# Layernorm, token-shift feed-forward and retention for 4096 tokens on one core: keys and values from one product, the token shift scaled by ScalarE

## The chip, the core and the metric

The kernel runs on one core of a Trainium2 chip. The metric is device time in microseconds, the median of the runs. A core has five engines that run their own instruction streams and wait for one another by semaphores: TensorE (PE in the profile; its weight loads are PEld), VectorE (DVE), ScalarE (ACT), GpSimd (POOL) and SyncE (SP), which starts the transfers.

## What is computed

x has 4096 tokens of 256 channels, in fp32. Three layers follow one another, each on the layernorm of its input (no gain, no bias) and added to it:

```python
x = x + 0.5 * ffn(layernorm(x))      # W_r, W_k, W_v, mu_r, mu_k
x = x + retention(layernorm(x))      # Wq, Wk, Wv, Wo, 8 heads of 32
x = x + 0.5 * ffn(layernorm(x))      # the same weights again

def ffn(x):                          # x_prev: the token before, zeros first
    xr = mu_r * x + (1.0 - mu_r) * x_prev
    xk = mu_k * x + (1.0 - mu_k) * x_prev
    r = sigmoid(xr @ W_r.T)
    return r * (square(relu(xk @ W_k.T)) @ W_v.T)
```

Retention is linear attention with a decay per head: within a chunk, scores q k^T are masked to the past and decayed and multiplied by v; a state of 32x32 per head carries the earlier chunks; the result goes through Wo.

## The kernel before

**Blocks and layers.** Tokens go in 16 blocks of 256 (TILES = 2 tiles of 128). Each block n passes the layers FFN1, RET and FFN2, which are staggered: in the steady loop (i from 6 to 15) TensorE works on FFN1 of one block, RET of a block two or three earlier and FFN2 of one earlier still. Chunks of the retention are 128 tokens, two per block (c = 0, 1).

**One layer's way.** VectorE takes the statistics (layer_stats), GpSimd the inverse deviation (inverse_std), ScalarE normalizes (normalize, L295), TensorE transposes (transpose_T, L890) so that channels lie on partitions, and ScalarE copies the result out of PSUM (evacuate_T, L302, with the last token of the block before as a halo, L305). For the token shift VectorE forms the difference of neighbouring tokens (difference, L536) and from it xk and xr (mix_k L545, mix_r L552: difference times mu plus the earlier token).

**Products in three passes.** Each fp32 operand is split in a high part in the reduced format fp32r and a low part with the rest (xk_high on ScalarE, xk_low on VectorE, xr_low on GpSimd L213, and so on), and a product is high x high + low x high + high x low. A half of a product is six matmuls with 256 columns, which half_T (L893) and half_rows (L901) issue: hidden, gate, ffn_out, query, key, value and retention_out each have two halves per block.

**Retention.** query and key come out with channels on partitions; VectorE scales the queries (decayed_query), ScalarE copies the keys to kT (evacuate_key). key_rows transposes kT back to rows, which VectorE scales to krow (decayed_key). value gives rows, which ScalarE copies to vrow (evacuate_value). scores (L976), each four row groups of 32 at once, are multiplied by a decay table (mask_scores, L607), intra (L1003) multiplies them by vrow, inter (L990) the queries by the state, outer (L1013) krow by vrow for the new state. Then o_high, o_low, retention_out, add_retention.

**Order.** Every engine's program is written out by hand as a list of such steps, with a start, the steady loop and an end; engines run their lists strictly in order. All eight PSUM banks are shared by several steps (B_T, B_HID and so on), and a step waits where its bank is still to be read. Loads of x, weights and tables are issued by SyncE at the start, stores as results come.

## Time and profile before

| | |
|---|---|
| median of 3 runs | 350.52 us (349.65 to 351.63) |
| the profiled execution | 349.89 us |
| its span, first to last instruction | 347.7 us |
| busy: PE, DVE, ACT, POOL | 325.6, 302.5, 211.5, 162.3 us |
| mean granted clock of TensorE | 0.990 |

Busy is the time in which at least one instruction of the engine ran. A matmul's record reaches beyond the start of the next one, since matmuls are pipelined; the rate is read from starts, not from the duration. An activation's or vector operation's record, too, can overlap the next one's start.

### The profile page before, as it was taken

What the parts mean: (1) busy time and instruction counts of PE and PEld (TensorE: products, weight loads), DVE (VectorE), ACT (ScalarE), POOL (GpSimd) and SP (SyncE); (2) the same over time, 40 slices, a digit from 0 to 9 for tenths busy, and PEclk for the clock granted to TensorE, in tenths of its full rate; (3) what the DMA queues carried; (4) which work ended last, traced back from release to release, by engine and by line L of the source; (5) the groups of instructions that cost most, each with busy time, mean ns of one, the idle gap of its engine ahead of it and who ended that gap; (6) DMA issues with size and microseconds to landing.
All of it is one profiled execution on the core that took longest, in us unless ns stands there. A gap on an engine that the chain in (4) does not pass through costs nothing.

```text
span 347.7 us, 10332 instructions
## 1 busy us (share of the span) xinstructions
PE 325.6 (94%) x3858; PEld 313.3 (90%) x3858; DVE 302.5 (87%) x695; ACT 211.5 (61%) x418; POOL 162.3 (47%) x271
## 2 busy tenths in 40 slices
PE   1969999899999999999999999999999999999774
PEld 1859999899999999999999999999999999999674
DVE  3898997999899998989899898989999897898744
ACT  3675557567667657657657757657756656545342
POOL 4384463435627281744727282653736181414130
PEclk9999999999999999999999999999999999999969
DMA  7601000000102020200202020100000000000001
GB/s 251 228 30 31 5 32 2 31 4 17 46 3 62 2 62 2 65 0 4 60 3 62 2 61 3 41 23 32 3 7 27 2 32 2 33 2 32 33 0 60
DMA packets 11664, 12.15 MB, mean 35 GB/s; under 512 B 992, under 2 KB 11232, under 8 KB 11616
## 3 DMA queue, kind: packets, MB, share of 16 engines
q1 hardware_dynamic: 11328, 11.44, 10.6%
q8 instruction: 31, 0.51, 0.6%
q14 instruction: 17, 0.14, 0.1%
q10 hardware_dynamic: 288, 0.07, 0.1%
HBM read 7.31 MB, written 4.19 MB: 33 GB/s over the span
## 4 chain that ended last, share of the span: by engine, by line
PE 85%; issue 6%; DVE 4%; POOL 2%; ACT 1%; DMA 1%; POOLq 0%; DVEq 0%; ACTq 0%
PE bank L906 36%; PE bank L898 24%; PE bank L890 6%; PE bank L976 5%; PE bank L990 5%; PE bank L1003 4%; PE bank L966 2%; PE bank L1013 2%; PE bank L1027 1%; DMA x<-in_x 1%; DVE stats L525 1%; POOL xr_lo L213 1%; POOL rstd L206 1%; DVE xk_lo L557 1%; DVE xrT L552 0%
## 5 line engine op out<-in xcount | busy, mean ns | idle before, releaser
L213 POOL TENSOR_TENSOR xr_lo<-xrT,xr_hi 128x512 fp32r<-128x512 f32 x32 | 54.3, 1697 | 95.4 <-ACT xr_hi L315 94.2
L295 ACT ACTIVATE xn<-x,shift,rstd 128x256 f32<-128x256 f32 x96 | 52.2, 593 | 12.4 <-POOL shift L209 12.4
L222 POOL TENSOR_TENSOR state_bd<-state,mask 128x256 f32<-128x256 f32 x32 | 28.6, 893 | 45.9 <-DVE state L621 43.9
L890 PE MATMUL bank<-ident,xn 128*128 128x128 f32 x192 | 30.5, 283 | 12.6 <-ACT xn L295 12.6
L607 DVE TENSOR_TENSOR attn<-bank,decay 128x512 f32<-128x512 f32 x64 | 40.5, 678 | 1.0 <-PE bank L976 0.4
L906 PE MATMUL bank<-w_hi,xr_hi 128*128 128x256 f32 x128 | 39.4, 308 | 0.4 <-POOL xr_lo L213 0.4
L525 DVE BATCH_NORM_STATS2 stats<-x 128x6 f32<-128x256 f32 x96 | 35.7, 414 | 4.6 <-DMA x<-in_x 4.4
L898 PE MATMUL bank<-xk_hi,w_hi 128*128 128x256 f32 x128 | 38.2, 299 | 0.9 <-DVE xk_lo L557 0.9
L906 PE MATMUL bank<-w_hi,ka_hi 128*128 128x256 f32 x128 | 36.8, 288 | 2.1 <-DVE ka_lo L563 2.1
L202 POOL TENSOR_TENSOR var_eps<-moments,eps 128x2 f32<-128x2 f32 x48 | 20.7, 431 | 38.3 <-DVE moments L529 38.1
L898 PE MATMUL bank<-xa_hi,w_hi 128*128 128x256 f32 x128 | 36.8, 287 | 0.0
L906 PE MATMUL bank<-w_lo,xr_hi 128*128 128x256 f32 x128 | 36.3, 284 | 0.0
L906 PE MATMUL bank<-w_hi,xr_lo 128*128 128x256 f32 x128 | 36.3, 284 | 0.0
L906 PE MATMUL bank<-w_lo,ka_hi 128*128 128x256 f32 x128 | 36.0, 281 | 0.0
L906 PE MATMUL bank<-w_hi,ka_lo 128*128 128x256 f32 x128 | 36.0, 281 | 0.0
L898 PE MATMUL bank<-xk_hi,w_lo 128*128 128x256 f32 x128 | 35.7, 279 | 0.0
L898 PE MATMUL bank<-xa_lo,w_hi 128*128 128x256 f32 x128 | 35.6, 278 | 0.0
L898 PE MATMUL bank<-xa_hi,w_lo 128*128 128x256 f32 x128 | 35.6, 278 | 0.0
L898 PE MATMUL bank<-xk_lo,w_hi 128*128 128x256 f32 x128 | 35.6, 278 | 0.0
L890 PEld LDWEIGHTS bank<-ident,xn 128*128 128x128 f32 x192 | 22.7, 145 | 13.7 <-issue 12.1
L206 POOL TENSOR_TENSOR rstd<-var_eps,exponent 128x2 f32<-128x2 f32 x48 | 33.6, 700 | 0.0
L570 DVE SCALAR_TENSOR_TENSOR gatedx<-bank,rgate 128x512 f32<-128x512 f32 x32 | 22.0, 687 | 12.6 <-PE bank L906 12.5
(80 smaller groups left out, 1068.4 us busy)
## 6 DMA issues: line engine op xcount, KB each, us to landing
x<-in_x SPq DMA_DIRECT2D x16, 256.0 KB, 3.0
x_out<-y SPq DMA_DIRECT2D x16, 256.0 KB, 2.6
w_f<-in_w SPq DMA_DIRECT2D x7, 256.0 KB, 5.2
decay<-in_decay SPq DMA_DIRECT2D x1, 512.0 KB, 6.3
decq<-in_decq SPq DMA_DIRECT2D x1, 256.0 KB, 5.8
deck<-in_deck SPq DMA_DIRECT2D x1, 256.0 KB, 6.0
mask<-in_mask SPq DMA_DIRECT2D x1, 128.0 KB, 5.5
ident<-in_ident ACTq DMA_DIRECT2D x1, 64.0 KB, 2.6
```

The costliest lines, as they stand in the source:

```text
L202: pool.tensor_tensor(var_eps[s][n % 2][:], m[:, :, 1], eps[:], ALU.add).then_inc(var_ready[s], 1)
L206: pool.tensor_tensor(rstd[s][n % 2][:], var_eps[s][n % 2][:], exponent[:], ALU.pow).then_inc(rstd_ready[s], 1)
L213: pool.tensor_tensor(xr_lo[f][n % 2][:], xrT[f][n % 2][:], xr_hi[f][n % 2][:].bitcast(F32), ALU.subtract).then_inc(xr_lo_ready[f], 1)
L222: pool.tensor_tensor(state_bd[1 - c][:], state[c][:].unsqueeze(2).broadcast_to([P, G, HG, HD]), mask[:], ALU.mult).then_inc(state_bd_ready ...
L295: act.activation(xn[s][n % 2][:, t, :], x[n % len(x)][:, t, :], ACT.Identity, bias=shift[s][n % 2][:, t:t + 1], scale=rstd[s][n % 2][:, t: ...
L525: dve.bn_stats(stats[s][n % 2][:, t, :], x[n % len(x)][:, t, :]).then_inc(stats_ready[s], 1)
L570: dve.scalar_tensor_tensor(out=gatedx[f][0][:], in0=halves(B_OUT[f]), scalar=0.5, in1=rgate[f][0][:], op0=ALU.mult, op1=ALU.mult).then_inc ...
L607: dve.tensor_tensor(attn[r][:], bank[B_SCORES[r]][:].rearrange("p (g c i) -> p g c i", g=G, c=TILES), decay[:, r, :, :].unsqueeze(2).broad ...
L890: mm = pe.transpose(halves(B_T[s])[:, g, t * P:(t + 1) * P], xn[s][n % 2][:, t, g * P:(g + 1) * P], ident[:])
L898: mm = pe.matmul(halves(b)[:, m, :], wt[:, g, cols], xt[:, g, :], start=(j == 0), stop=(j == 5))
L906: mm = pe.matmul(halves(b)[:, t, :], xt[:, g, cols], wt[:, g, :], start=(j == 0), stop=(j == 5))
L976: mm = pe.matmul(bank[B_SCORES[r]][:, group * P:(group + 1) * P], kT[rows, g, c * P:(c + 1) * P], qT[rows, g, c * P:(c + 1) * P], start=Tr ...
```

## The change

Keys and values are computed by one product: their weights lie side by side (wkv_hi, wkv_lo, 512 columns), and key_value streams 512 columns in each of 2 x 6 matmuls per block, into two adjacent banks, one per tile. Keys now come out as rows. VectorE scales them to krow first (decayed_key), ScalarE then copies the values (evacuate_value waits for krow_ready), and key_T transposes krow to kT, so that the scores already hold the decay of the keys; mask_scores multiplies by a causal table of zeros and ones [128, 128] instead of a decay table per head.

For the token shift ScalarE forms mu * x for both mixes out of PSUM (scale_k, scale_r: two activations of 128x256 each), beside the plain copy; VectorE's difference is gone, and mix_k and mix_r are (1 - mu) times the earlier token plus that product. mu_rest = 1 - mu is computed once on GpSimd.

PSUM banks are assigned anew, and all four engines' orders are new. Which engine splits which weight at the start has changed too. relu also waits for ka_hi_ready of the block before. At the start ScalarE's list begins split_high_act(W_K), normalize(FFN1, 0), evacuate_T, scale_k, scale_r (all FFN1, 0), normalize(FFN1, 1); TensorE's is hidden(0) both halves, gate(0, 0), hidden(1, 0), gate(0, 1), ffn_out(0). At the end the copy of xnT of block 15 is followed by scale_k and scale_r. The new steady loops of GpSimd, ScalarE, VectorE and TensorE (in this order, each under its own `for i in range(6, 16)`) are shown below, the last three without the lines that they replace.

```diff
-        w_hi = [sb(f"w_hi_{w}", [G, D], F32R) for w in range(7)]
-        w_lo = [sb(f"w_lo_{w}", [G, D], F32R) for w in range(7)]
+        w_hi = [None if w in (W_KEY, W_VAL) else sb(f"w_hi_{w}", [G, D], F32R)[:] for w in range(7)]
+        w_lo = [None if w in (W_KEY, W_VAL) else sb(f"w_lo_{w}", [G, D], F32R)[:] for w in range(7)]
+        wkv_hi, wkv_lo = sb("wkv_hi", [G, 2 * D], F32R), sb("wkv_lo", [G, 2 * D], F32R)
+        for side, w in enumerate((W_KEY, W_VAL)):
+            w_hi[w] = wkv_hi[:, :, side * D:(side + 1) * D]
+            w_lo[w] = wkv_lo[:, :, side * D:(side + 1) * D]
...
-        B_T = {FFN1: 4, RET: 1, FFN2: 5}
-        B_HID, B_GATE, B_OUT = {FFN1: 0, FFN2: 4}, {FFN1: 2, FFN2: 2}, {FFN1: 6, FFN2: 7}
-        B_Q, B_KEY, B_VAL, B_KROW = 7, 5, 3, 5
-        B_SCORES = (4, 7, 6, 1)
-        B_OT, B_U, B_Y = 5, (3, 0), 3
+        B_T = {FFN1: 7, RET: 4, FFN2: 6}
+        B_HID, B_GATE, B_OUT = {FFN1: 2, FFN2: 3}, {FFN1: 1, FFN2: 0}, {FFN1: 5, FFN2: 2}
+        B_Q, B_KV, B_KEYT = 1, 6, 7
+        B_SCORES = (4, 3, 7, 5)
+        B_OT, B_U, B_Y = 0, (1, 5), 0
...
+        def keys_values(which):
+
+            return psum[:, B_KV:B_KV + TILES, :].rearrange("p t (k c) -> p t k c", k=2)[:, :, which, :]
+
...
             for i in range(6, 16):
                 inverse_std(FFN1, i)
-                spread_state(0, i - 4)
+                spread_state(1, i - 4)
                 xr_low(FFN2, i - 5)
+                xr_low(FFN1, i - 1)
                 inverse_std(FFN2, i - 4)
-                xr_low(FFN1, i - 1)
                 inverse_std(RET, i - 2)
-                spread_state(1, i - 4)
+                spread_state(0, i - 3)
...
+            def scale_k(f, n):
+                if n == 0:
+                    act.wait_ge(mu_loaded, 16)
+                act.wait_ge(xnT_psum[f], n + 1)
+                act.wait_ge(xk_ready[f], max(2 * (n - 1), 0))
+                for g in range(G):
+                    act.activation(akT[f][n % 2][:, g, :], halves(B_T[f])[:, g, :], ACT.Copy, scale=mu[:, 1, g:g + 1]).then_inc(ak_ready[f], 1)
+
+            def scale_r(f, n):
+                if n == 0:
+                    act.wait_ge(mu_loaded, 16)
+                act.wait_ge(xnT_psum[f], n + 1)
+                act.wait_ge(xr_ready[f], max(2 * (n - 1), 0))
+                for g in range(G):
+                    act.activation(arT[f][n % 2][:, g, :], halves(B_T[f])[:, g, :], ACT.Copy, scale=mu[:, 0, g:g + 1]).then_inc(ar_ready[f], 1)
+
...
             def xa_high(n):
                 act.wait_ge(xnT_psum[RET], n + 1)
-                act.wait_ge(val_psum, n)
+                act.wait_ge(q_psum, n)
                 act.activation(xa_hi[:], halves(B_T[RET]), ACT.Copy).then_inc(xa_hi_ready, 1)
 
             def evacuate_key(n):
-                act.wait_ge(key_psum, n + 1)
+                act.wait_ge(keyT_psum, n + 1)
                 act.wait_ge(scores_psum, HG * n)
-                act.activation(kT[:], halves(B_KEY), ACT.Copy).then_inc(key_ready, 1)
+                act.activation(kT[:], halves(B_KEYT), ACT.Copy).then_inc(key_ready, 1)
 
             def evacuate_value(n):
-                act.wait_ge(val_psum, n + 1)
+                act.wait_ge(krow_ready, n + 1)
                 act.wait_ge(u_psum[1], n)
                 act.wait_ge(intra_done, n)
-                act.activation(vrow[:], halves(B_VAL), ACT.Copy).then_inc(val_ready, 1)
+                act.activation(vrow[:], keys_values(1), ACT.Copy).then_inc(val_ready, 1)
...
             for i in range(6, 16):
+                evacuate_value(i - 4)
+                relu(FFN2, i - 6)
+                square(FFN2, i - 6)
+                square_high(FFN2, i - 6)
+                evacuate_key(i - 4)
+                relu(FFN1, i - 2)
+                normalize(FFN2, i - 5, x2)
+                square(FFN1, i - 2)
+                sigmoid(FFN2, i - 6)
+                square_high(FFN1, i - 2)
+                evacuate_T(FFN2, i - 5)
+                scale_k(FFN2, i - 5)
+                normalize(RET, i - 3, x1)
+                xk_high(FFN2, i - 5)
+                o_high(i - 4)
+                scale_k(FFN1, i - 1)
+                xa_high(i - 3)
+                scale_r(FFN2, i - 5)
+                evacuate_T(FFN1, i - 1)
+                scale_r(FFN1, i - 1)
+                xr_high(FFN2, i - 5)
+                sigmoid(FFN1, i - 2)
+                xk_high(FFN1, i - 1)
                 normalize(FFN1, i, x0)
                 xr_high(FFN1, i - 1)
...
             def mix_k(f, n):
+                dve.wait_ge(ak_ready[f], 2 * n + 2)
                 dve.wait_ge(xnT_ready[f], n + 1)
                 dve.wait_ge(halo_ready[f], n)
                 dve.wait_ge(xk_lo_ready[f], max(n - 1, 0))
                 for g in range(G):
-                    dve.scalar_tensor_tensor(out=xkT[f][n % 2][:, g, :], in0=dT[f][n % 2][:, g, :], scalar=mu[:, 1, g:g + 1],
-                                             in1=xnT[f][n % 2][:, g, 0:BT], op0=ALU.mult, op1=ALU.add).then_inc(xk_ready[f], 1)
+                    dve.scalar_tensor_tensor(out=xkT[f][n % 2][:, g, :], in0=xnT[f][n % 2][:, g, 0:BT], scalar=mu_rest[:, 1, g:g + 1],
+                                             in1=akT[f][n % 2][:, g, :], op0=ALU.mult, op1=ALU.add).then_inc(xk_ready[f], 1)
 
             def mix_r(f, n):
-                dve.wait_ge(d_ready[f], n + 1)
+                if n == 0:
+                    dve.wait_ge(halo_zeroed, 2)
+                    dve.wait_ge(mu_rest_set, 1)
+                dve.wait_ge(ar_ready[f], 2 * n + 2)
+                dve.wait_ge(xnT_ready[f], n + 1)
+                dve.wait_ge(halo_ready[f], n)
                 dve.wait_ge(xr_lo_ready[f], max(n - 1, 0))
                 for g in range(G):
-                    dve.scalar_tensor_tensor(out=xrT[f][n % 2][:, g, :], in0=dT[f][n % 2][:, g, :], scalar=mu[:, 0, g:g + 1],
-                                             in1=xnT[f][n % 2][:, g, 0:BT], op0=ALU.mult, op1=ALU.add).then_inc(xr_ready[f], 1)
+                    dve.scalar_tensor_tensor(out=xrT[f][n % 2][:, g, :], in0=xnT[f][n % 2][:, g, 0:BT], scalar=mu_rest[:, 0, g:g + 1],
+                                             in1=arT[f][n % 2][:, g, :], op0=ALU.mult, op1=ALU.add).then_inc(xr_ready[f], 1)
 
 ...
             def decayed_key(n):
                 if n == 0:
                     dve.wait_ge(deck_loaded, 16)
-                dve.wait_ge(krow_psum, n + 1)
-                dve.wait_ge(u_psum[0], n)
+                dve.wait_ge(kv_psum, TILES * n + TILES)
                 dve.wait_ge(u_psum[1], n)
-                dve.tensor_tensor(krow[:], halves(B_KROW), deck[:], ALU.mult).then_inc(krow_ready, 1)
+                dve.tensor_tensor(krow[:], keys_values(0), deck[:], ALU.mult).then_inc(krow_ready, 1)
 
             def mask_scores(r, n):
                 if n == 0:
-                    dve.wait_ge(decay_loaded, 16)
+                    dve.wait_ge(causal_loaded, 16)
                 dve.wait_ge(scores_psum, HG * n + r + 1)
                 dve.wait_ge(intra_done, n)
-                dve.tensor_tensor(attn[r][:], bank[B_SCORES[r]][:].rearrange("p (g c i) -> p g c i", g=G, c=TILES),
-                                  decay[:, r, :, :].unsqueeze(2).broadcast_to([P, G, TILES, P]), ALU.mult).then_inc(attn_ready[r], 1)
+                dve.tensor_tensor(attn[r][:], bank[B_SCORES[r]].rearrange("p (k i) -> p k i", i=P),
+                                  causal[:].unsqueeze(1).broadcast_to([P, G * TILES, P]), ALU.mult).then_inc(attn_ready[r], 1)
...
+            for i in range(6, 16):
                 add_retention(i - 5)
                 scale_state(0, i - 4)
+                xk_low(FFN1, i - 2)
+                decayed_key(i - 4)
                 layer_stats(FFN2, i - 5, x2)
                 add_ffn1(i - 3)
                 decayed_query(i - 4)
                 layer_stats(RET, i - 3, x1)
                 square_low(FFN2, i - 6)
+                mask_scores(2, i - 4)
+                update_state(0, i - 4)
+                mask_scores(0, i - 4)
+                mask_scores(1, i - 4)
+                mask_scores(3, i - 4)
                 layer_stats(FFN1, i, x0)
                 mix_k(FFN2, i - 5)
+                scale_state(1, i - 4)
+                gate(FFN2, i - 6)
+                update_state(1, i - 4)
+                square_low(FFN1, i - 2)
+                xk_low(FFN2, i - 5)
+                o_low(i - 4)
+                xa_low(i - 3)
+                mix_r(FFN2, i - 5)
+                mix_k(FFN1, i - 1)
+                mix_r(FFN1, i - 1)
+                add_ffn2(i - 6)
+                gate(FFN1, i - 2)
...
+            def key_value(n, t):
+
+                if n == 0:
+                    weight_split(n, W_KEY)
+                    weight_split(n, W_VAL)
+                pe.wait_ge(xa_lo_ready, n + 1)
+                cols = slice(t * P, (t + 1) * P)
+                passes = [(xa_hi, wkv_hi), (xa_hi, wkv_lo), (xa_lo, wkv_hi)]
+                for j, (g, (xt, wt)) in enumerate([(g, p) for g in range(G) for p in passes]):
+                    mm = pe.matmul(bank[B_KV + t], xt[:, g, cols], wt[:, g, :], start=(j == 0), stop=(j == 5))
+                mm.then_inc(kv_psum, 1)
+
+            def key_T(n):
+                pe.wait_ge(krow_ready, n + 1)
+                for g in range(G):
+                    for c in range(TILES):
+                        mm = pe.transpose(halves(B_KEYT)[:, g, c * P:(c + 1) * P], krow[:, c, g * P:(g + 1) * P], ident[:])
+                mm.then_inc(keyT_psum, 1)
...
             for i in range(6, 16):
                 pe.wait_ge(gated[FFN2], i - 5)
+                hidden(FFN1, i - 1, 0)
+                pe.wait_ge(krow_ready, i - 2)
+                pe.wait_ge(val_ready, i - 2)
+                key_T(i - 3)
+                query(i - 3, 1)
+                pe.wait_ge(xout_ready[RET], i - 3)
+                gate(FFN2, i - 5, 0)
+                hidden(FFN1, i - 1, 1)
+                pe.wait_ge(xa_lo_ready, i - 2)
                 pe.wait_ge(relu_ready[FFN2], i - 4)
+                pe.wait_ge(key_ready, i - 2)
+                pe.wait_ge(gated[FFN1], i - 1)
+                scores(i - 3, 1, first=True)
+                scores(i - 3, 3)
+                scores(i - 3, 2)
+                scores(i - 3, 0, last=True)
+                pe.wait_ge(q_ready, i - 2)
+                outer(0, i - 3)
+                gate(FFN2, i - 5, 1)
+                pe.wait_ge(krow_ready, i - 2)
+                pe.wait_ge(val_ready, i - 2)
+                transpose_T(FFN2, i - 4)
+                pe.wait_ge(attn_ready[2], i - 2)
                 transpose_T(FFN1, i)
+                pe.wait_ge(relu_ready[FFN1], i)
+                ffn_out(FFN2, i - 5, 0)
                 pe.wait_ge(gate_ready[FFN2], i - 4)
+                inter(0, i - 3)
+                pe.wait_ge(state_ready[0], i - 2)
                 gate(FFN1, i - 1, 0)
+                ffn_out(FFN2, i - 5, 1)
+                intra(i - 3)
+                pe.wait_ge(attn_ready[3], i - 2)
+                outer(1, i - 3)
+                inter(1, i - 3)
+                gate(FFN1, i - 1, 1)
+                pe.wait_ge(attn_ready[0], i - 2)
+                transpose_T(RET, i - 2)
+                pe.wait_ge(state_ready[1], i - 2)
+                ffn_out(FFN1, i - 1, 0)
                 pe.wait_ge(attn_ready[1], i - 2)
+                hidden(FFN2, i - 4, 0)
+                pe.wait_ge(o_lo_ready, i - 2)
+                retention_out(i - 3, 0)
+                ffn_out(FFN1, i - 1, 1)
+                pe.wait_ge(ak_ready[FFN2], 2 * (i - 3))
+                pe.wait_ge(ar_ready[FFN2], 2 * (i - 3))
                 pe.wait_ge(xnT_ready[FFN2], i - 3)
+                key_value(i - 2, 0)
+                retention_out(i - 3, 1)
+                pe.wait_ge(ar_ready[FFN1], 2 * (i + 1))
+                key_value(i - 2, 1)
+                hidden(FFN2, i - 4, 1)
+                pe.wait_ge(gate_ready[FFN1], i)
+                query(i - 2, 0)
             pe.wait_ge(gated[FFN2], 11)
```

## Rows read from the trace of the kernel before

**Rows 1.** The page's busy times and its slices of the span, TensorE's row (tenths busy in each of 40).
```profile
PE 325.6 (94%) x3858; PEld 313.3 (90%) x3858; DVE 302.5 (87%) x695; ACT 211.5 (61%) x418; POOL 162.3 (47%) x271
PE   1969999899999999999999999999999999999774
```

**Rows 2.** The page's chain of work that ended last, shares by engine.
```profile
PE 85%; issue 6%; DVE 4%; POOL 2%; ACT 1%; DMA 1%; POOLq 0%; DVEq 0%; ACTq 0%
```

**Rows 3.** Stretches: us, busy us and instructions of each engine, PE clock, DMA share, GB/s.
```profile
0.00:20.00 20.00, 10.47 (x62) 9.84 (x62) 13.19 (x29) 10.69 (x20) 9.59 (x26) 1.00 0.61 208
20.00:40.00 20.00, 17.80 (x218) 16.56 (x219) 17.48 (x42) 12.44 (x25) 11.91 (x17) 1.00 0.10 29
...
80.00:99.74 19.74, 19.74 (x242) 19.16 (x242) 18.36 (x44) 12.93 (x26) 10.23 (x16) 1.00 0.10 29
...
317.00:333.00 16.00, 11.46 (x150) 10.35 (x149) 10.96 (x23) 7.34 (x14) 4.35 (x9) 0.94 0.06 19
333.00:347.70 14.70, 10.12 (x79) 9.34 (x77) 7.05 (x14) 4.90 (x9) 2.01 (x2) 0.83 0.10 36
```

**Rows 4.** The timeline of TensorE from 182 to 202 us (start, duration).
```profile
182.01 0.60 PE L890 MATMUL bank<-ident,xn 128*128 128x128 f32 x4
...
195.01 0.60 PE L890 MATMUL bank<-ident,xn 128*128 128x128 f32 x4
195.37 0.36 PE L898 MATMUL bank<-xk_hi,w_hi 128*128 128x256 f32 x1
195.57 0.28 PE L898 MATMUL bank<-xk_hi,w_lo 128*128 128x256 f32 x1
...
200.33 0.28 PE L898 MATMUL bank<-xa_hi,w_hi 128*128 128x256 f32 x1
...
201.63 0.28 PE L898 MATMUL bank<-xa_lo,w_hi 128*128 128x256 f32 x1
201.75 0.60 PE L890 MATMUL bank<-ident,xn 128*128 128x128 f32 x4
```

**Rows 5.** The timeline of TensorE in the last block, at the lower clock.
```profile
335.01 0.41 PE L906 MATMUL bank<-w_hi,xr_hi 128*128 128x256 f32 x1
...
337.36 0.41 PE L906 MATMUL bank<-w_hi,xr_lo 128*128 128x256 f32 x1
```

**Rows 6.** Groups by line: shapes, count, busy us, mean ns, idle time before.
```profile
L295 ACT ACTIVATE xn<-x,shift,rstd 128x256 f32<-128x256 f32 x96 | 52.2, 593 | 12.4 <-POOL shift L209 12.4
...
L563 DVE TENSOR_TENSOR ka_lo<-sqT,ka_hi 128x512 fp32r<-128x512 f32 x32 | 26.0, 813 | 3.8 <-ACT sqT L324 3.3 <-ACT ka_hi L329 0.5
...
L536 DVE TENSOR_TENSOR dT<-xnT 128x512 f32<-128x512 f32 x32 | 22.0, 687 | 1.7 <-ACT xnT L305 1.0 <-ACT xnT L302 0.7
...
L302 ACT ACTIVATE xnT<-bank 128x512 f32<-128x512 f32 x32 | 19.1, 596 | 22.4 <-PE bank L890 22.3
...
L615 DVE TENSOR_TENSOR state_dec<-state,gstate 128x64 f32<-128x64 f32 x32 | 6.9, 217 | 0.1
...
L305 ACT ACTIVATE xnT<-xnT 128x2 f32<-128x2 f32 x30 | 6.1, 202 | 0.0
```

**Rows 7.** The timelines of ScalarE and VectorE in the steady loop.
```profile
196.18 1.09 ACT L295 ACTIVATE xn<-x,shift,rstd 128x256 f32<-128x256 f32 x2
197.17 0.62 ACT L310 ACTIVATE xk_hi<-xkT 128x512 fp32r<-128x512 f32 x1
...
197.08 0.68 DVE L585 TENSOR_TENSOR xa_lo<-bank,xa_hi 128x512 fp32r<-128x512 f32 x1
197.68 1.66 DVE L552 SCALAR_TENSOR_TENSOR xrT<-dT,mu,xnT 128x256 f32<-128x256 f32 x4
199.26 0.68 DVE L557 TENSOR_TENSOR xk_lo<-xkT,xk_hi 128x512 fp32r<-128x512 f32 x1
```

**Rows 8.** The timelines of ScalarE and TensorE in the last block.
```profile
331.11 1.09 ACT L295 ACTIVATE xn<-x,shift,rstd 128x256 f32<-128x256 f32 x2 [0.92 <-POOL shift L209]
...
332.34 1.09 PE L890 MATMUL bank<-ident,xn 128*128 128x128 f32 x4 [3.45 <-ACT xn L295]
```

955 lines of the change are left out of this document (420 added, 535 removed).

## The prediction

> **What bounds the kernel now.** I read the page's totals first [rows 1]: TensorE is busy for 94% of the span, VectorE for 87%, ScalarE for 61%, and TensorE's slices are full from the ninth to the 37th of 40. The chain that ended last says the same by another way: 85% of it is TensorE [rows 2]. The table of stretches then shows where that holds [rows 3]. Between 80 and 99.74 us TensorE is busy for all 19.74 us. Idle time lies at the start (9.5 us of the first 20), in the ramp (2.2 us of the next 20) and at the end (4.5 us before 333 us, 4.6 us after it). The first transposes of block 6 and those of block 7 start 19.74 us apart (182.01 and 201.75 us) [rows 4], so that one block of 256 tokens costs one period of 19.74 us, and nothing but TensorE's own stream sets it. Sixteen blocks of this are 316 of the 347.7 us. What shortens that stream is therefore worth its full size in every block, as long as no loop through the other engines becomes longer than the new period.
>
> The profiled execution took 349.89 us, 2.2 us more than its span. The sum below is made against it; the median of the runs shown, 350.52 us, lies 0.6 us above it, and I move the result by as much. I count a difference under 0.5% (1.75 us) as no change, since the three runs before already differ by 2 us.
>
> **Keys and values in one product.** Before, key and value are four halves of six matmuls with 256 columns each, 24 per block. After, key_value is twice six matmuls with 512 columns. As many columns are streamed; 12 weight loads and 12 starts fall away. In a run of twelve, the 256-column matmuls start 0.118 us apart ((201.63 - 200.33) / 11) [rows 4], where 256 columns at 2.4 GHz are 0.107 us. So 0.011 us of each is not streaming. Is it a fixed part that a matmul twice as wide pays once, not at all, or does it grow with the columns? The tail answers half of it: at a lower granted clock (0.83 in the mean of that stretch [rows 3]) eleven starts take 2.35 us, 0.2136 us each [rows 5], which is 256 columns at 1.2 GHz (0.2133) with nothing left over. The extra time vanishes when streaming lasts 0.213 us; it looks like a floor on the interval between two matmuls, not like a surcharge. 512 columns at 2.4 GHz last 0.213 us as well, so I take 0.215 us. The bounds are 0.213 us (streaming alone) and 0.236 us (all of it grows with the columns). Saved per block: 24 x 0.118 - 12 x 0.215 = 0.25 us, between 0 and 0.28; over 16 blocks 4.0 us, between 0 and 4.4.
>
> The Trainium skill (TensorE: Matmul & The Clock Gate, section "Wait — 56ns, not 53.3ns?") gives a start-to-start time of N / 2.4 GHz plus about 2.5 ns. That speaks against this change: two 256-column matmuls would take 218 ns and one of 512 columns 216 ns, a gain of 0.03 us per block and 0.5 us in all instead of 4.0. The trace does not bear it out at 256 columns (118 ns, not 109) [rows 4]; for 512 columns it agrees with what I take.
>
> **The new order on TensorE.** A group of transposes takes 0.36 us, and the first matmul after it takes 0.20 us to the next instead of 0.118 (195.01, 195.37, 195.57) [rows 4]: leaving the fp32 operations costs 0.08 us. In the new steady loop transpose_T(FFN2) and transpose_T(FFN1) stand side by side, and outer(0) behind scores; inter(0) stands alone. Counted group by group one exit less remains, some 0.1 us a block (0 to 0.15), 1 us in all. key_T replaces key_rows: four transposes for four. The new period of TensorE is 19.74 - 0.25 - 0.1 = 19.39 us.
>
> **ScalarE.** scale_k and scale_r add eight activations of 128x256 out of PSUM per block. The trace has none of the form. A copy of 128x512 out of PSUM takes 0.596 us and one of two columns 0.202, so 0.77 ns a column, and 256 columns without operands come to 0.40 us; normalize, with a scale and a bias per partition, takes 0.593 [rows 6], so each operand costs about 0.1. One operand: 0.50 us, and since two normalizations occupy the engine for 0.99 us though each lasts 0.593 [rows 7], 0.1 overlaps: 0.40 us each. Bounds: 0.30 (the operand free) and 0.50 (as normalize). That is 3.2 us more on 12.93 us of ScalarE in a period [rows 3], 16.1 of 19.39: 83%, hidden behind TensorE by load.
>
> **VectorE.** difference goes: two of 0.69 us a block [rows 6], 0.60 in a packed queue [rows 7]. mix_k and mix_r keep their form. mask_scores reads one causal table instead of a decay table per head, in the same shape; I cost it and decayed_key, which now reads two banks, at nothing, as they keep 512 elements. VectorE falls from 18.36 to 17.2 us a period, 88%; GpSimd stays where it is. These 1.2 us are worth nothing by themselves: VectorE was not the bound. The decay table, 512 KB among the first loads, shrinks to 64 KB; nothing waited on it.
>
> **The loop that could replace TensorE.** Values are now evacuated only after krow is ready, and key_T waits for both, with hidden(FFN1, 0) alone between the last query half and it. I followed the loop once round. TensorE from key_T to the end of inter(1) holds seven halves (six matmuls each) and all fp32 groups but transpose_T(RET). A half is 6 x 0.118 = 0.71 us; of the period before, 20 halves are 14.18 us, which leaves 5.56 for the fp32 groups, of which 0.44 is the group left out and 0.1 falls away: 4.96 + 5.02 = 9.98 us. Then release 0.28 (the transposes' 0.60 lasts 0.24 beyond the next start [rows 4]), o_high 0.50 (0.596 less the overlap of 0.1), scale_k(FFN1) 0.80, xa_high 0.50, scale_r(FFN2) 0.90 with its end: 3.0 us. VectorE is then packed: three mixes at 0.79 (four instructions take 1.58 [rows 7]), add_ffn2, gate and add_retention at 0.60, scale_state 0.13 (0.217 long [rows 6]), xk_low 0.60, decayed_key 0.68: 5.6 us. evacuate_value 0.60 and two handoffs, 0.14 of them from ScalarE to TensorE (332.20 to 332.34) [rows 8]: 0.8 us. Together 19.3 to 19.4 us, against 19.39 of TensorE; I take 19.3. It fits, with hardly 0.1 us to spare. The queues around it fit too: evacuate_key follows 0.8 us ahead of scores, ka_lo and xk_lo of both layers some 0.8 us ahead of their products.
>
> **Start and end.** At the start ScalarE has four more activations before normalize(1) (1.6 us), so the second transposes come 1.5 us later; but hidden(1) moves ahead of ffn_out(0), whose wait for ka_lo stood there, and counted step by step scores(0) come as early as before, within half a microsecond. I cost start and ramp at +0.5 us (-1 to +2): each early block has a longer ScalarE path and little other work to hide it. In the last block the copy of xnT is followed by scale_k (0.9) where difference (0.7) was: equal within 0.2. The wait before the last transposes (3.45 us [rows 8]) starts earlier, because o_high and o_low of block 15 no longer queue behind xk_high, the sigmoid and more; I take -0.5 us (-1.5 to +1).
>
> **Sum.** -4.0 (wide product) - 1.0 (exits) + 0.5 (ramp) - 0.5 (end) = -5.0 us: span 342.7, profiled execution 344.9, median **345.5 us**.
>
> **Rivals.** (a) The value loop sets the period and eats the gain. If a scale costs 0.50 us like a normalization, four of them lie in the loop: 19.3 + 0.4 = 19.7 us, as before. Some 12.5 periods gain 0.5 us in all, the ramp about 1: 349. For it: 0.1 us of slack. Against: the sum has one operand less than normalize. 12%.
> (b) Slower: GpSimd and VectorE disturb each other in that loop. square_low, an operation of the shape of xk_low, takes 0.81 us in the mean for 0.68 undisturbed [rows 6, 7]. xr_low of both layers now runs just while the packed VectorE part does. If three of its operations are stretched by 0.3 us, the period is 20.2 us: 0.46 x 12.5 - 1.2 = +4.5 us, 355. It decides from 0.7 us of stretch on; below 0.44 it costs only gain. 10%.
> (c) A 512-column matmul takes 0.236 us: only exits are won, 349.5. Rows 5 speak against it. 5%.
> (d) Ramp and end lose 3 to 4 us by the longer ScalarE path, for instance because TensorE waits in blocks 1 to 3: 349. 5%.
> (e) The floor between two matmuls is all that counts and a wide one takes hardly more than 0.118 us: TensorE's period would be 19.39 - 12 x 0.097 = 18.2, the value loop would hold at 19.3, and 16 x 0.44 = 7 us would go: 343.5. At the low clock a column never took less than one clock [rows 5]. 2%. The Trainium skill (same page, section "Back-to-back issue gap") states this 131 ns for 512 columns as a sustained rate; no run here shows it.
>
> **Numbers.** The forecast holds 66% and reaches from 342.5 (0.28 and 0.15 a block are 6.9 us, and 1 of the good bounds at start and end) to 348.5. To leave out 2 in 10 at most, the range goes to 350: it takes in (a), (c) and (d). Faster by over 0.5% is the forecast and (e), 68%; within it (a), (c) and (d), 22%; slower (b), 10%.
>
> **What would show it.** Matmuls of 512 columns start 0.215 us apart; periods of 19.4 us wholly filled; ScalarE near 83% and VectorE at 88% in them; scale instructions of 0.50 us; no wait of TensorE for vrow or krow at key_T. Wrong would be: a wait at key_T in every period, for ScalarE's evacuation of the values; a pitch of 0.236; or more idle time of TensorE than 22 us.

## The result: slower, by 3.6%

| | before | after |
|---|---|---|
| median | 351.07 us (349.65 to 352.94, 4 runs) | **362.60 us** (361.35 to 364.68, 4 runs) |
| ratio | | 1.0355, interval 1.0306 to 1.0404 |
| span of the profiled execution | 347.7 us | 360.7 us |
| time of the first scores of blocks 0, 2, 3, 12 | 33.99, 67.33, 87.08, 264.74 | 37.68, 71.60, 92.18, 277.63 |
| period from block 3 to 12 | 19.74 us | 20.58 us (one of 20.81) |

The ratio and its interval are those on record for these runs; the two medians alone give 1.033, which lies in the same interval. Three runs with a granted clock of 0.56 to 0.66 are left out of all times and ratios below: one of pool_apart (536.36 us), one of start_order (464.82 us) and one of the kernel before beside it (534.43 us).

The forecast was 345.5 us, range 342.5 to 350. The time lies outside it, on the side of rival (b), which had 10%.

The last two lines say where the 13.0 us of span come from: the first scores begin 3.7 us late, the ramp to block 3 adds 1.4, nine steady periods add 7.8, and from the scores of block 12 on less than 0.1 is added. So there are two losses, one ahead of block 3 and one in every period.

### The profile after

The page's busy times and TensorE's slices, to be read beside [rows 1]:

```profile
PE 332.8 (92%) x3666; PEld 309.3 (86%) x3666; DVE 303.5 (84%) x664; ACT 257.3 (71%) x546; POOL 150.0 (42%) x271
PE   1879999999999999999999999999999999999764
PEclk9998999999999999999999999999999999999988
```

In tenths the slices look as full as before; a loss of 2% in each can't be seen in them. The page's chain of work that ended last shows it at once, 60% TensorE where it was 85% [rows 2]:

```profile
PE 60%; DVE 15%; issue 13%; ACT 9%; DMA 1%; POOL 1%; DVEq 0%; ACTq 0%
```

Stretches, columns as in [rows 3]; the third is one period:

```profile
0.00:20.00 20.00, 10.60 (x56) 10.06 (x56) 10.31 (x25) 11.36 (x23) 8.99 (x26) 1.00 0.57 185
20.00:40.00 20.00, 17.33 (x149) 15.50 (x149) 15.92 (x39) 15.00 (x31) 11.01 (x20) 0.91 0.09 29
...
80.00:100.58 20.58, 20.16 (x231) 18.80 (x229) 18.91 (x42) 15.73 (x35) 9.31 (x17) 1.00 0.08 27
...
333.00:360.70 27.70, 17.23 (x164) 15.96 (x162) 14.80 (x30) 13.47 (x28) 5.89 (x8) 0.90 0.09 30
```

TensorE has 0.42 us without any instruction in the period, besides gaps hidden in the overlap of records. VectorE is busy for 18.91 us though the change took 1.2 us of work from it: it should be 17.2. The 0.91 in the second line is TensorE at 1.2 GHz from 27.6 to 31.0 us, behind a wait of 1.93 us for ka_lo that ended at 26.95.

Groups by line, columns as in [rows 6]:

```profile
L223 POOL TENSOR_TENSOR xr_lo<-xrT,xr_hi 128x512 fp32r<-128x512 f32 x32 | 42.7, 1334 | 76.2 <-ACT xr_hi L342 76.2
L608 DVE SCALAR_TENSOR_TENSOR xrT<-xnT,mu_rest,arT 128x256 f32<-128x256 f32 x64 | 40.5, 674 | 0.1
L596 DVE SCALAR_TENSOR_TENSOR xkT<-xnT,mu_rest,akT 128x256 f32<-128x256 f32 x64 | 29.2, 497 | 6.1 <-ACT akT L324 3.8 <-ACT xnT L316 2.1 <-issue 0.2
L332 ACT ACTIVATE arT<-psum,mu 128x256 f32<-128x256 f32 x64 | 27.7, 503 | 0.0
L324 ACT ACTIVATE akT<-psum,mu 128x256 f32<-128x256 f32 x64 | 26.8, 476 | 1.1 <-PE psum L902 1.1
L378 ACT ACTIVATE vrow<-psum 128x512 f32<-128x512 f32 x16 | 9.6, 598 | 42.3 <-DVE krow L655 42.3
```

The reader is to see two lines of equal form, xrT and xkT, with 674 and 497 ns: something stretches the one and not the other. ScalarE's scales last 0.48 to 0.50 us. Its wait for krow ahead of vrow is 2.6 us in each of 16 blocks; with the loop repaired (pool_apart and three_together, below) 1.4 to 1.5 us of it are left, so the late part of it is 1.2 us. VectorE's timeline where that happens, one period of 20.58:

```profile
184.68 0.88 DVE L608 SCALAR_TENSOR_TENSOR xrT<-xnT,mu_rest,arT 128x256 f32<-128x256 f32 x2
185.79 0.88 DVE L596 SCALAR_TENSOR_TENSOR xkT<-xnT,mu_rest,akT 128x256 f32<-128x256 f32 x2 [0.23 <-issue]
186.59 1.96 DVE L608 SCALAR_TENSOR_TENSOR xrT<-xnT,mu_rest,arT 128x256 f32<-128x256 f32 x2
...
190.27 0.39 DVE L670 TENSOR_TENSOR state_dec<-state,gstate 128x64 f32<-128x64 f32 x1
190.58 0.68 DVE L613 TENSOR_TENSOR xk_lo<-xkT,xk_hi 128x512 fp32r<-128x512 f32 x1
191.19 0.68 DVE L655 TENSOR_TENSOR krow<-psum,deck 128x512 f32<-128x512 f32 x1
```

and GpSimd's in the same stretch:

```profile
186.56 1.31 POOL L223 TENSOR_TENSOR xr_lo<-xrT,xr_hi 128x512 fp32r<-128x512 f32 x1 [3.61 <-ACT xr_hi L342]
189.28 1.29 POOL L223 TENSOR_TENSOR xr_lo<-xrT,xr_hi 128x512 fp32r<-128x512 f32 x1 [1.42 <-ACT xr_hi L342]
```

xrT started 0.03 us after GpSimd's xr_lo and took 1.96 us instead of 0.88. Between the second xr_lo and VectorE's steps on PSUM (gatedx, x) nothing is stretched; state_dec, at its very end, is (0.39 for 0.22). Behind this queue stand krow, then vrow on ScalarE, then TensorE, which waits twice in the period, for xk_lo and, after vrow, ahead of key_T:

```profile
191.41 0.36 PE L910 MATMUL psum<-xk_hi,w_hi 128*128 128x256 f32 x1 [0.39 <-DVE xk_lo L613]
...
192.59 0.63 PE L974 MATMUL psum<-ident,krow 128*128 128x128 f32 x4 [0.23 <-issue]
```

TensorE's own rows of the wide product, to be read beside [rows 4]:

```profile
188.25 0.39 PE L967 MATMUL psum<-wkv_lo,xa_hi 128*128 128x512 f32 x1
188.48 0.39 PE L967 MATMUL psum<-wkv_hi,xa_lo 128*128 128x512 f32 x1
188.71 0.40 PE L967 MATMUL psum<-wkv_hi,xa_hi 128*128 128x512 f32 x1
188.95 0.40 PE L967 MATMUL psum<-wkv_lo,xa_hi 128*128 128x512 f32 x1
```

They start 0.233 us apart ((188.95 - 188.25) / 3, and as much in the mean of the 120 between 80 and 280 us), not 0.215. In the last block the transposes wait 3.53 us and run at 1.2 GHz, as in [rows 5, 8]:

```profile
345.47 1.09 PE L902 MATMUL psum<-ident,xn 128*128 128x128 f32 x4 [3.53 <-ACT xn L306]
```

### The profile page after: what moved, and what is told of

It reads as the page before. It is cut to its first block, busy times and chain, and to the rows that moved or that the text cites. A ratio compares the mean times of both kernels' runs of the same rounds, so it can differ in the third digit from the quotient of the medians.

```text
span 360.7 us, 10193 instructions
## 1 busy us (share of the span) xinstructions
PE 332.8 (92%) x3666; PEld 309.3 (86%) x3666; DVE 303.5 (84%) x664; ACT 257.3 (71%) x546; POOL 150.0 (42%) x271
## 4 chain that ended last, share of the span: by engine, by line
PE 60%; DVE 15%; issue 13%; ACT 9%; DMA 1%; POOL 1%; DVEq 0%; ACTq 0%
PE psum L918 19%; PE psum L910 13%; PE psum L902 5%; PE psum L984 5%; PE psum L998 5%; PE psum L1011 4%; DVE xrT L608 4%; PE psum L967 4%; ACT akT L324 3%; PE psum L974 3%; ACT arT L332 3%; DVE x L686 2%; DVE y L637 2%; DVE xk_lo L613 2%; PE psum L1021 2%
## 5 line engine op out<-in xcount | busy, mean ns | idle before, releaser
L662 DVE TENSOR_TENSOR attn<-psum,causal 128x512 f32<-128x512 f32 x64 | 40.8, 682 | 3.9 <-PE psum L984 3.8
L918 PE MATMUL psum<-w_hi,ka_hi 128*128 128x256 f32 x128 | 39.3, 307 | 3.2 <-DVE ka_lo L619 3.2
L608 DVE SCALAR_TENSOR_TENSOR xrT<-xnT,mu_rest,arT 128x256 f32<-128x256 f32 x64 | 40.5, 674 | 0.1
L918 PE MATMUL psum<-w_hi,xr_hi 128*128 128x256 f32 x128 | 40.2, 314 | 0.0
L910 PE MATMUL psum<-xk_hi,w_hi 128*128 128x256 f32 x128 | 38.0, 296 | 2.5 <-DVE xk_lo L613 2.5
L918 PE MATMUL psum<-w_hi,ka_lo 128*128 128x256 f32 x128 | 36.6, 286 | 0.0
L910 PE MATMUL psum<-xk_hi,w_lo 128*128 128x256 f32 x128 | 36.6, 286 | 0.0
L910 PE MATMUL psum<-xk_lo,w_hi 128*128 128x256 f32 x128 | 36.5, 285 | 0.0
L918 PE MATMUL psum<-w_lo,ka_hi 128*128 128x256 f32 x128 | 36.5, 285 | 0.0
L918 PE MATMUL psum<-w_lo,xr_hi 128*128 128x256 f32 x128 | 36.3, 283 | 0.0
```

The source lines that it names most:

```text
L608: dve.scalar_tensor_tensor(out=xrT[f][n % 2][:, g, :], in0=xnT[f][n % 2][:, g, 0:BT], scalar=mu_rest[:, 0, g:g + 1], in1=arT[f][n % 2][:, ...
L662: dve.tensor_tensor(attn[r][:], bank[B_SCORES[r]].rearrange("p (k i) -> p k i", i=P), causal[:].unsqueeze(1).broadcast_to([P, G * TILES, P ...
L910: mm = pe.matmul(halves(b)[:, m, :], wt[:, g, cols], xt[:, g, :], start=(j == 0), stop=(j == 5))
L918: mm = pe.matmul(halves(b)[:, t, :], xt[:, g, cols], wt[:, g, :], start=(j == 0), stop=(j == 5))
```

## The experiments

Theory: GpSimd and VectorE shut each other out in the value loop, and TensorE waits for what is late by it (the steady loss). Rivals: the wide product or ScalarE's scales cost the time by themselves; the loop is too long even without collisions. Ratios are to the kernel before, measured beside each group of runs (349.46, 349.05, 349.34, 349.88 us).

### What sets the period

**pool_apart**: GpSimd's two xr_low apart, the first behind a VectorE step after which VectorE reads PSUM.

```diff
                 spread_state(1, i - 4)
+                pool.wait_ge(xout_ready[FFN2], i - 5)
                 xr_low(FFN2, i - 5)
-                xr_low(FFN1, i - 1)
                 inverse_std(FFN2, i - 4)
                 inverse_std(RET, i - 2)
+                xr_low(FFN1, i - 1)
                 spread_state(0, i - 3)
```

> The changed kernel, in the steady loop of GpSimd alone: xr_low(FFN2) waits until add_ffn2 of VectorE is through, so that it runs beside gate and add_retention, which read PSUM; xr_low(FFN1) comes behind inverse_std(RET), beside mask_scores. Theory A (mix_r(FFN1) takes 1.96 us instead of 0.88 because GpSimd's xr_low holds VectorE up, and this lies in the loop that sets the period): mix_r(FFN1) back to 0.9 us, the period from 20.8 to 19.9 us, the time 350 to 353 us. Theory B (the loop is set by ScalarE's longer queue; mix_r waits for its inputs anyway): no change, 361 to 364 us.

Measured 354.20 us, ratio 1.0139 (1.0095 to 1.0182). The period is 19.76 us, wholly filled by TensorE, and mix_r(FFN1) is undisturbed:

```profile
183.60 0.88 DVE L609 SCALAR_TENSOR_TENSOR xrT<-xnT,mu_rest,arT 128x256 f32<-128x256 f32 x2
```

Making one GpSimd step wait and moving the other, with no work taken away, gives back the whole steady loss. The time lies 1.2 us above what was expected because of the start: in the profiled execution block 1 of x came late (its statistics began at 7.31 us, 5.89 in the changed kernel), and the first scores with it (38.77 against 37.68).

**key_first**: VectorE does what TensorE waits for first (with gate(FFN1) moved behind the turn of the loop).

```diff
+                xk_low(FFN1, i - 2)
+                decayed_key(i - 4)
+                if i > 6:
+                    gate(FFN1, i - 3)
                 add_retention(i - 5)
                 scale_state(0, i - 4)
-                xk_low(FFN1, i - 2)
-                decayed_key(i - 4)
```

> The changed kernel, in VectorE's steady loop xk_low(FFN1) and decayed_key moved ahead of gate(FFN1), add_retention and scale_state. Theory A (TensorE waits for xk_lo and for the values behind krow, both of which stand behind these three): these three (1.6 us) leave the loop, TensorE is filled again, period 19.8 to 19.9 us, 350 to 353 us. Theory B (the wait moves to gate or add_retention, which others need as much): less than 0.3 us a period, above 359 us.

Measured 353.92 us (0.9 above what was expected), 1.0119 (1.0089 to 1.0148), period 19.76. Here the collision is still there (xrT takes 1.95 us), but three steps that nobody waits for, 1.3 us, now stand behind krow instead of ahead of it. Two independent ways of winning back some 1.2 us in the loop do the same.

**scale_early**: ScalarE's scale_k(FFN1) ahead of o_high, to let VectorE's mixes start earlier.

> The changed kernel, in ScalarE's steady loop scale_k(FFN1) moved ahead of o_high, where ScalarE stands idle for 1.19 us of each period. Theory A (o_high, scale_k, xa_high, scale_r lie one behind the other in the loop that sets the period): 0.5 to 0.7 us less in each of ten periods, 355 to 358 us. Theory B (the loop does not pass through ScalarE there): no change, 361 to 364 us.

Measured 361.98 us, 1.0348 (1.0319 to 1.0377): hardly anything, period 20.52. Theory A missed. ScalarE's wait ahead of o_high falls from 1.19 to 0.46 us, but xa_high now waits 0.56 us for the transposes of RET, which stand behind inter(1) on TensorE. Two ways lead from TensorE back into this loop, and with the one shortened the other is nearly as long: 0.06 us a period are won.

**narrow_kv**: the changed kernel, key_value again in pairs of 256 columns.

> The changed kernel with key_value in 24 matmuls of 256 columns instead of 12 of 512, everything else as it is. Theory A (the period of 20.8 us is a loop through ScalarE and VectorE, and 512 columns at 0.234 us cost what two times 256 cost, 0.117 us each): the time stays within 0.5%, 361 to 364 us. Theory B (the wide product itself costs the time, by its pitch or because 512 columns in one piece delay what follows): 2% or more faster, 355 us or less. Theory C (the wide product does save start intervals): slower by 2 us or more.

Measured 362.21 us, 1.0357 (1.032 to 1.0393), period 20.57: undoing the wide product costs nothing. As TensorE waits in this loop anyway, that alone says little of its price; the pitch does, next.

**pitch_alone** leaves the computation out: matmuls in a row, first alone, then with VectorE and ScalarE streaming SBUF to SBUF.

> Not the computation at all: one block is loaded and stored 16 times, and TensorE runs fp32r matmuls alone: 80 and 60 with 256 columns, 40 with 512, 60 with 128, then 90 with 256 and 40 with 512 while VectorE and ScalarE stream 128x512 in SBUF. Theory A (the rate at the high clock is what 0.118 for 256 and 0.234 us for 512 columns say, a cost per column): 512 columns at 0.23 us and 256 at 0.115 even with nothing beside them. Theory B (neighbours take bandwidth): 0.107 and 0.213 us alone, 0.117 and 0.234 with VectorE and ScalarE at work. Theory C (a floor of the interval): 256 at 0.118, 512 at 0.214.

Alone, 512 columns start 0.227 us apart, 256 columns 0.120, 128 columns 0.111; with the neighbours at work 0.227 and 0.120, so they don't matter here. None of the three theories fits. From 256 to 512 columns the pitch grows by 0.107 us, what 256 columns take at 2.4 GHz (0.1067); so about 0.014 us stay over at either width, a surcharge once per matmul. A wide matmul saves that much per pair of narrow ones by itself; 512 columns are far from 0.215. In the kernels not even that is left: 0.233 against twice 0.1166.

**difference_back**: no scales on ScalarE, VectorE's difference again directly ahead of mix_k, everything else as changed.

> The changed kernel with the token shift as before: VectorE's difference directly ahead of mix_k, no scale_k and scale_r on ScalarE, the rest and all orders as changed. Theory A (the loop holds scale_k and scale_r, 1.6 us, on ScalarE; one difference of 0.6 us takes their place, the collision with GpSimd stays): about 0.3 to 1 us less a period, 352 to 359 us. Theory B (ScalarE's scaling is the whole cost): 350 us. Theory C (VectorE is the bound): slower than 362 us.

Measured 377.99 us, 1.0821 (1.08 to 1.0843). A miss: period 21.79 us, VectorE busy for 20.57 of it, TensorE waits 1.4 us each time for xk_lo:

```profile
102.00:123.80 21.80, 20.20 (x230) 18.83 (x230) 20.57 (x44) 13.17 (x26) 9.56 (x16) 1.00 0.08 26
```

The scales are thus not the loss in the loop: without them it is 1.2 us longer. Its trace shows two parts. One difference (0.60 in a packed queue) stands ahead of krow, and the collisions are worse:

```profile
193.52 1.91 DVE L557 SCALAR_TENSOR_TENSOR xkT<-akT,mu,xnT 128x256 f32<-128x256 f32 x2
197.95 1.09 DVE L626 TENSOR_TENSOR state_dec<-state,gstate 128x64 f32<-128x64 f32 x1
```

The mix is stretched by 1.03 us, in the changed kernel by 1.08; but state_dec, 0.22 us long, now takes 1.09 where the changed kernel had 0.39: it started 0.26 us after a second xr_lo. So this run doesn't price the scales alone.

**scale_in_before**: the kernel before with the scales alone (its own order and products; the scales stand ahead of the plain copy).

> The kernel before with the scaling by ScalarE alone: evacuate_T also writes mu times x for both mixes (in place of xk and xr), mix_k and mix_r add (1 - mu) times the earlier token, difference is gone; orders and the narrow products as before. Theory A (the scaling costs only where the queue behind it lies in a loop; before's order leaves more room): TensorE stays filled in most of the steady loop, 350 to 354 us. Theory B (ScalarE's longer path is what makes the changed kernel slow in any order): 358 us or more.

Measured 362.38 us, 1.0347 (1.0301 to 1.0392), as theory B had it, but TensorE stays filled, as theory A had it; the period is 19.97 us:

```profile
80.00:99.97 19.97, 19.97 (x242) 19.38 (x241) 17.49 (x43) 15.63 (x35) 9.10 (x16) 1.00 0.09 28
```

Its first scores come 4.5 us late, those of block 3 7.7, and from block 12 on it loses another 3.8: I read this as ScalarE's longer path, which the old order doesn't hide in start, ramp and end, but no run separates it. The other 0.23 us in each period lies in the matmuls' pitch, below. That the scales cost this much in any order is refuted by start_apart, below, which has them and is level.

**three_together**: pool_apart, key_first and scale_early in one.

> The three order edits together (GpSimd's xr_low apart, scale_k(FFN1) ahead of o_high, xk_low and decayed_key ahead of gate(FFN1)). Theory A: the loop through ScalarE and VectorE is some 3 us shorter than TensorE's stream, so TensorE alone sets the period. With 512 columns at 0.234 us its stream is what it was before: 19.7 to 19.8 us a period, 349 to 352 us, level with the kernel before. Theory C (the wide product or the new grouping does shorten the stream by 0.3 us once nothing waits): 345 us or less.

Measured 352.76 us (0.8 above what was expected), 1.0102 (1.0085 to 1.0119), span 350.9, period 19.76 and full:

```profile
80.00:99.76 19.76, 19.76 (x230) 18.73 (x229) 17.49 (x42) 15.84 (x35) 9.56 (x16) 1.00 0.10 28
```

The steady loss is gone; 3.2 us of span remain, all there by the first scores (37.34 against 33.99 us).

### The collision by itself

**ports_alone** leaves the computation out: twelve VectorE operations of each kind, alone and with GpSimd subtracting beside them.

> Not the computation: VectorE and GpSimd alone on 128x512 fp32, in phases of 12 operations, the output is a copy of the first block. First VectorE by itself: subtraction of two SBUF tiles, of a PSUM bank and an SBUF tile, scalar_tensor_tensor of two SBUF tiles, copy. Then GpSimd by itself, subtracting two SBUF tiles. Then each of the four VectorE phases again with GpSimd's subtractions beside it. Theory (VectorE operations with two SBUF operands and GpSimd's shut each other out): VectorE alone 0.6 to 0.7 us per subtraction and GpSimd alone 1.2 to 1.3; together, the two-SBUF phases take as long as both in sum (a subtraction and its GpSimd neighbour some 1.9 us together), while the phase with a PSUM operand runs at its own 0.6 to 0.7, GpSimd at 1.3. Rival, that both only share bandwidth of SBUF: each slows by some tens of per cent in all phases, the PSUM one less. The copy (one SBUF operand) is open: 0.39 alone; shut out too if the fast mode of a single operand takes the same way in.

VectorE's timeline; the first four rows are alone, the last four beside GpSimd:

```profile
17.42 7.31 DVE L67 TENSOR_TENSOR vc<-va,vb 128x512 f32<-128x512 f32 x12 [11.72 <-DMA x_out<-xin]
24.65 7.26 DVE L70 TENSOR_TENSOR vc<-bank,vb 128x512 f32<-128x512 f32 x12
31.83 8.03 DVE L73 SCALAR_TENSOR_TENSOR vc<-va,vs,vb 128x512 f32<-128x512 f32 x12
39.78 4.11 DVE L76 COPY vc<-va 128x512 f32<-128x512 f32 x12
53.86 20.08 DVE L67 TENSOR_TENSOR vc<-va,vb 128x512 f32<-128x512 f32 x12 [9.98 <-POOL pc L113]
73.86 7.25 DVE L70 TENSOR_TENSOR vc<-bank,vb 128x512 f32<-128x512 f32 x12
88.76 20.07 DVE L73 SCALAR_TENSOR_TENSOR vc<-va,vs,vb 128x512 f32<-128x512 f32 x12 [7.65 <-POOL pc L113]
108.75 15.83 DVE L76 COPY vc<-va 128x512 f32<-128x512 f32 x12
```

Per operation: two SBUF tiles 0.61 us alone, 1.67 beside GpSimd; scalar_tensor_tensor 0.67 and 1.67; one operand in PSUM 0.60 and 0.60; a copy, one SBUF operand, 0.34 and 1.32 (1.40 without the first of the twelve, which still ran alone). GpSimd's subtraction starts every 1.22 us alone and beside the PSUM operand, and every 1.67 beside two SBUF tiles. 1.67 is nearly 0.61 + 1.22, and both engines keep that one pace: they take turns, whole operation by operation. The PSUM operand leaves both undisturbed. That the plain copy is shut out too I had left open. The Trainium skill (GPSIMD Engine Reference, section "Specifications") says that GpSimd shares its SBUF interfaces with VectorE, with contention for instructions in a two-port mode or with two SBUF inputs. The runs agree for two SBUF inputs and give the price: 1.0 to 1.1 us for each VectorE operation beside a GpSimd subtraction of 1.22.

### Where the start goes

**value_weight**: three_together, with the split of W_VAL a few steps earlier, VectorE's high part and GpSimd's low part, of which the second is shown.

```diff
             xr_low(FFN1, 1)
+            split_low(pool, W_VAL)
             inverse_std(RET, 0)
             inverse_std(FFN1, 3)
-            split_low(pool, W_VAL)
```

> The three reorderings of the steady loop (three_together) plus one edit of the start: VectorE's split_high(W_VAL) goes four steps up, behind mix_r(FFN1, 1), and GpSimd's split_low(W_VAL) goes two steps up, ahead of inverse_std(RET, 0). In three_together TensorE waited 1.21 us for wkv_lo ahead of the first key_value product (31.24 us). Theory 1, that the start's loss is a chain whose last link is this weight: key_value(0) begins at 30.0 instead of 31.2, the first scores at 36.1 instead of 37.34, and the span is 1.2 shorter, 349.7, the time 351.5. Rival, that the start's loss is set elsewhere and the ramp behind it absorbs a later or earlier first block: the time stays within 0.4 of three_together's 352.76. Second rival: GpSimd's split now runs beside VectorE's two-operand steps at 23 us and stretches them, so that RET's statistics come later and nothing is gained.

The profiled execution behaves as expected, first scores 1.4 us and span 1.7 us earlier (35.94, 349.2). The median does not: 353.12 us (351.17 to 353.86), 1.0109 (1.009 to 1.0129), and the profiled one is the fastest of four. In its trace the gain is the edit's. The statistics of block 1 of x began 0.8 us earlier than in three_together's (5.57 against 6.34), but T(1), the transposes of that block, began at the same time (12.14, 12.18), and so did those of RET (27.70, 27.73). Only then the wait of 1.21 us for wkv_lo is gone and the first product of keys and values starts 1.4 us earlier (29.86 against 31.24). Why the three other runs keep nothing of it no trace shows, so the edit is inconclusive by its time.

**start_order**: three_together, with the first steps of block 0 and 1 reordered on TensorE, ScalarE and VectorE, and the warming matmuls put where TensorE waited.

```diff
-            keep_warm(0, 8)
+            keep_warm(0, 14)
             pe.wait_ge(ar_ready[FFN1], 2)
             transpose_T(FFN1, 1)
-            keep_warm(0, 10)
+            keep_warm(0, 4)
...
             xk_high(FFN1, 0)
+            xr_high(FFN1, 0)
             scale_k(FFN1, 1)
             evacuate_T(FFN1, 1)
-            xr_high(FFN1, 0)
-            xk_high(FFN1, 1)
+            scale_r(FFN1, 1)
             relu(FFN1, 0)
             square_high(FFN1, 0)
             square(FFN1, 0)
-            scale_r(FFN1, 1)
+            xk_high(FFN1, 1)
...
```

> three_together plus the order of the start up to 25 us: TensorE's 8 and 10 warming matmuls become 14 and 4 (none is left out, they stand where TensorE waited 1.51 us for xn), gate(0) and ffn_out(0) go ahead of hidden(1); ScalarE does xr_high(0) right behind xk_high(0), relu(0) and the squares of block 0 ahead of xk_high(1), sigmoid(0) ahead of the split of W_KEY, the squares of block 1 ahead of evacuate_T(2) and scale_k(2); VectorE splits W_V while it waits and does square_low(0) ahead of xk_low(1). In three_together hidden(0) began at 15.19 (before 13.66) and ran its first four matmuls at the clock's lower level (0.21 us each), ffn_out(0) began at 19.98 (before 17.87), the RET transpose at 27.73 (before 25.90). Theory 1, that the change's start is late because ScalarE's four scale activations and the later T(1) push hidden(0), relu(0) and with them every first result back: hidden(0) at 13.9 at full clock, ffn_out(0) at 18, the RET transpose at 25.5 to 26; key_value(0) still waits for wkv_lo, so the span is 1 to 1.8 shorter than three_together's, time 351 to 351.8. Rival, that the ramp absorbs it: 352.4 to 353.1.

Measured 351.31 us, 1.0054 (1.0036 to 1.0071); first scores at 35.37, span 349.1. What the first scores gain, 2.0 us, the end gains nearly whole (1.8). In it VectorE's add_ffn1(0) meets GpSimd's xr_low, which began at 19.97 us:

```profile
20.10 1.70 DVE L633 TENSOR_TENSOR x<-x,gatedx 128x512 f32<-128x512 f32 x1
```

**start_both**: both edits (the W_VAL split now ahead of xr_low(1)).

> Both edits of the start together, on top of the three reorderings of the loop (the split of W_VAL: high part on VectorE behind xk_low(1), low part on GpSimd ahead of xr_low(1)). Theory 1, that the whole of the 3.2 us that three_together's span still lies above before's comes from the start: key_value(0) begins at 27.5 to 28.5 (before: key(0) at 27.98), the first scores at 33.5 to 34.5 (before 33.99, three_together 37.34), the period stays 19.76, the span is 347 to 348.5, the time 349 to 350.5, level with the kernel before. Rival, that the ramp from one block to all three layers absorbs an earlier first block (VectorE and ScalarE are the bound there): the first scores come early, scores(3) does not, and the time is 352 or more.

Measured 351.97 us (350.4 to 353.36), 1.0067 (1.0044 to 1.0091): a miss, no better than start_order. The profiled execution is the slowest of six. Block 1 of x came late (its statistics began at 6.95 us instead of 5.51 in start_order), GpSimd had the split of W_R queued ahead of inverse_std(1), and T(1) began 0.6 us later than in start_order, behind a wait of 0.78 us; the twelve matmuls of hidden(0) after them ran at 1.2 GHz (0.213 us each until 16.9 us). add_ffn1(0) takes 1.70 us again.

**start_apart**: the same, with inverse_std(1) ahead of the split of W_R and xr_low(1) behind add_ffn1(0).

```diff
+            inverse_std(FFN1, 1)
             split_low(pool, W_R)
-            inverse_std(FFN1, 1)
...
+            pool.wait_ge(xout_ready[FFN1], 1)
             xr_low(FFN1, 1)
```

> start_both plus two edits of GpSimd's start: inverse_std(FFN1, 1) goes ahead of split_low(W_R), and xr_low(FFN1, 1) waits until VectorE's add_ffn1(0) is done. Theory (the start's loss is collisions of GpSimd with VectorE and GpSimd's own queue): add_ffn1(0) takes 0.69 instead of 1.70 us, T(1) no longer waits with the arrival of block 1 for a weight split, the RET transpose comes at 25.3 to 25.9 (start_order 26.51, before 25.90), key_value(0) at 27.3 to 28.2, the first scores at 33.4 to 34.3, the span is 347.2 to 348.2 and the time 348.8 to 350.2, level with the kernel before. Rival, that the remainder is the longer way through ScalarE's scale activations and through krow, vrow, key_T and kT ahead of the first scores: the first scores stay at 35 or later and the time at 351 or more.

Measured **349.65 us** (349.28 to 350.48, 12 runs), before 349.88 (349.27 to 351.7): ratio 0.9992 (0.9976 to 1.0009). First scores at 34.29 us, span 347.6. add_ffn1(0) takes 0.69 us, and the spread of the runs falls to 1.2 us. With its loop and its start reordered, and with all the work of the change in it, the changed kernel is level with the one before.

**start_alone**: that start on the changed kernel's own loop.

> The changed kernel with the start of start_apart and its own loop (none of the three reorderings). If loop and start are separate losses that add up, the span is the changed kernel's 360.7 less what start_apart gains on three_together (350.9 to about 347.7): 357.5, the time 359 to 360, the period 20.58. If the loop absorbs an earlier start (its own waits set the pace from the first block on), the time is 361.5 or more.

Measured 358.96 us, 1.025 (1.0216 to 1.0284), period 20.58, span 357.9. The two losses nearly add up:

| | loop as changed | loop reordered |
|---|---|---|
| start as changed | 362.6 | 352.8 |
| start reordered | 359.0 | 349.7 |

### Where TensorE's own saving went

With a full TensorE the period is 19.76 us against 19.74, where 19.39 was expected. I sorted the start-to-start times of eight periods by kind, three_together against the kernel before. The groups that are no products (transposes, scores, intra, inter, outer), with the steps into and out of them, take 5.74 us instead of 5.89; the first matmuls after such a group 1.24 instead of 1.25; the twelve wide matmuls 2.80, exactly what 24 narrow ones took. But 256-column matmuls start 0.1166 us apart in the kernel before (80 to 280 us), and 0.119 in the changed one, its variants and scale_in_before: 84 such steps a period are +0.19 us, which cancels the 0.17 that the new grouping saves.

The mean of 0.1166 hides two paces. A third of those steps in the kernel before take 0.114 us, in stretches of up to 16 matmuls at the same place of every period, and the others 0.118; in the changed kernel and scale_in_before 5 to 9% are so short and the others take 0.119.

**pitch_psum** leaves the computation out: do reads of PSUM by others slow TensorE?

> Not the computation: runs of 120 matmuls of 256 columns, the output is a copy of the first block. First with no other engine at work; then with ScalarE copying 512 columns out of PSUM (another bank), with ScalarE scaling 256 columns out of PSUM, with VectorE subtracting out of PSUM, with both, and with ScalarE copying from SBUF to SBUF. Theory, that reads of PSUM by other engines take turns from TensorE's writes: the quiet pitch and the one beside the SBUF copy are equal, and the pitch beside the scales is 0.002 to 0.004 us longer, the one beside both longer still. Rival, that the 2% between the kernels lies in what TensorE's own stream holds (which operands and banks follow one another): all pitches are equal within 0.001.

Stretches with matmuls counted: alone, beside ScalarE's copies, its scales, VectorE, both, and ScalarE from SBUF.

```profile
19.00:31.00 12.00, 12.00 (x102) 1.00 0.00 0
33.00:45.00 12.00, 12.00 (x103) 1.00 0.00 0
46.00:55.00 9.00, 9.00 (x77) 1.00 0.01 2
61.00:72.00 11.00, 11.00 (x94) 1.00 0.01 1
75.00:84.00 9.00, 9.00 (x78) 1.00 0.01 2
90.00:102.00 12.00, 12.00 (x103) 1.00 0.00 1
```

The mean step is 0.120 us in all six: reads of PSUM are not it. Since scale_in_before keeps TensorE's stream and has the longer pitch all the same, the operands and their order, the rival, are not it either. This 2% stays open.

## Why the prediction was wrong

**What bounded the kernel: right.** TensorE's period sets the kernel before; in the changed one it is full again only with the loop repaired (19.76 us).

**Keys and values in one product: wrong.** The step "it looks like a floor on the interval between two matmuls, not like a surcharge" failed. I inferred it from the lower clock [rows 5]; 512 columns measured 0.233 us in the kernel, near the bound 0.236 of rival (c), and 0.227 alone, where the 0.014 us over streaming are a surcharge. The term of -4.0 us is 0.0. The 0.118 was also taken from one stretch of twelve; the mean of the kernel before is 0.1166. At the lower clock something else may hide the surcharge; no run says what.

**The exits: right.** The new grouping saves 0.17 us a period (0.1, bounds 0 to 0.15), but the longer pitch of the 256-column matmuls costs 0.19: net +0.02 us a period. This cost was in none of my terms.

**ScalarE: right.** 0.48 to 0.50 us for a scale (0.50), two in 0.83 to 0.89 (0.90 with the end), and 15.7 to 15.8 us busy a period (16.1).

**VectorE: right in work, wrong in use.** Without the collisions in the loop 17.49 us a period (17.2); as changed 18.91. One xk_low in each period of three_together still takes 1.23 us, off the path.

**The value loop: the step that failed.** "It fits, with hardly 0.1 us to spare" counted every VectorE operation in it undisturbed. So it does fit, as far as runs show: pool_apart fills 19.76; whether it would have fitted 19.39 no run shows. My count of the loop was 19.3; the measured stretch in it is 1.08 for xrT and 0.17 for state_dec: 19.3 + 1.25 = 20.55, measured 20.58. That the two agree to 0.03 is partly luck, as the count is an estimate. Rival (b) had the mechanism and the place right, and its size at 0.9; its threshold of 0.7 us was not tested. I gave it 10% because square_low's mean of 0.81 us looked like a small disturbance. The single ones show more: of its 32 operations in the kernel before nine take 1.00 us and one 1.50, and of GpSimd's 32 xr_lo eleven take 2.41 us instead of 1.29. And the count of slack should have set the chance: with 0.1 us of slack, one meeting decides.

**Start and ramp: the second step that failed.** I took +0.5 (-1 to +2); it is +3.7 at the first scores and +5.1 at block 3, of which start_alone gives back 3.5 at either place, and some 1.5 at block 3 are the loop's, as they are still there with that start. "Counted step by step scores(0) come as early as before" left out GpSimd's queue (W_VAL's low part: 1.2 us of waiting in three_together) and its encounters with VectorE. Rival (d) had this size for 5%, but put it to ScalarE's longer path. difference_back, without the scales on ScalarE, has its first scores at 37.10 us, only 0.6 earlier (VectorE does the difference there instead). That several causes share the 3.0 to 3.5 us is shown; how much each has is not separated, as value_weight was inconclusive and start_order moved steps of three engines at once.

**The end: nearly right.** -0.5 (-1.5 to +1); under +0.1 from block 12 on, the last wait 3.53 against 3.45 us [rows 8].

## What to carry to other kernels

Before moving GpSimd work, list VectorE's operations beside it: where both have SBUF operands only, the one that comes second waits until the other is through (here 1.1 us), while VectorE's subtractions and mixes with an operand in PSUM cost nothing; put those beside GpSimd. A loop through four engines with 0.1 us of slack is to be costed with one such meeting in it. And what a wider matmul saves is to be taken from a stream of both widths, not inferred from the lower clock.

## What the runs showed of the hardware

- Who waits is the one that comes second. In the kernel before it was GpSimd: its xr_lo, 0.03 us behind xk_lo, took 2.41 us instead of 1.29, and waited out y as well, while VectorE ran both from SBUF without a stretch. After, it was VectorE, 0.03 us behind xr_lo. The same meeting, once free and once on the path. The kernel before:

```profile
179.53 0.69 DVE L557 TENSOR_TENSOR xk_lo<-xkT,xk_hi 128x512 fp32r<-128x512 f32 x1
179.56 2.41 POOL L213 TENSOR_TENSOR xr_lo<-xrT,xr_hi 128x512 fp32r<-128x512 f32 x1 [6.00 <-ACT xr_hi L315]
```

- A copy of 128x512 with one SBUF operand, 0.34 us alone, takes 1.40 us beside GpSimd's subtractions.
- A matmul's pitch (start to start, fp32r) is 0.111 us for 128 columns, 0.120 for 256 and 0.227 for 512 alone at the full clock: from 256 to 512 columns it grows by the streaming alone, below that hardly at all.
- The 256-column pitch differs by 2% between kernels (0.1166 and 0.119), and reads of PSUM by other engines don't cause it.
- A first block's lateness reaches the end almost undiminished (start_order: 2.0 us at the first scores, 1.8 in the span). But block 1 of x can be late for a while at no cost: with its statistics at 5.57 or at 6.34 us, T(1) began at 12.14 and 12.18; at 7.31 it began at 13.00.
